# Scatters in pairs with work between them, and a final sum taken in another order

## The chip, the cores and the metric

The kernel runs on one core of a Trainium2 chip, as one launch. The metric is device time in microseconds (us). The engines are TensorE (PE; its weight loads are PEld), VectorE (DVE), ScalarE (ACT), GpSimd (POOL) and SyncE (SP, which only issues DMAs here). They run side by side, each in its own program order, and wait for each other by semaphores.

## The reference

The input x is 4 batches of 256 tokens of 256 values, all f32. Two layers follow, each with a layer norm before and behind it and a residual sum:

```
x = x + layernorm(attention(layernorm(x)))          16 heads of 128, rope, causal softmax
x = x + layernorm(experts(layernorm(x)))
experts(x): logits = x @ router.T + bias; the best 4 of 16 experts per token, weights by softmax
            out = sum over those 4 of weight * (down(gated(gate_up(x))) + down_bias)
layernorm(x) = (x - mean) / sqrt(var + 1e-5)        over the 256 values of a token
```

## The kernel before

Attention runs first, batch by batch and head by head (64 slots `n`). The expert layer works on tiles of 128 rows, one expert each. Which tokens go to which expert is only known at run time, so the kernel sorts rows in DRAM.

**Scatter.** For each of the 8 tiles of 128 tokens, GpSimd issues four indirect DMAs (`scatter(t, k)`, L530) that write the normalised rows `xrow` into `rows_d`, sorted by expert. Tiles 0 to 5 are scattered during attention, one or two DMAs per head. Tiles 6 and 7, the last batch, are scattered by eight DMAs in a row after attention.

**Tiles.** There are 47 expert tiles. The first 9 (`EARLY`) are full already without the last batch and are planned early. The others need the table of the last batch: VectorE works it out in `plan_tiles` (L1105 to L1122), TensorE turns it (L1519), VectorE stores it (`table_out`, L1126). SyncE then waits for that table and for all 32 scatters before it loads tile 9 (`load_rows`, L456). For each tile TensorE turns the rows (`turn_tile`, L1528), multiplies by the gate and up weights (`gate_up`, L1544) and by the down weights (`down`, L1563). ScalarE copies the turned rows (`xgT_out`, through the helper at L649), copies half of the weights into `gu_now` (also L649), applies the gelu (L759) and weighs the result into a ring `y` of 6 buffers (`weigh`, L777). VectorE copies the other half of the weights (`place_gu`, L1146, which waits for the `gate_up` of two tiles before), and does the clamping (L1156, L1162) and the product (L1172).

**Sums.** GpSimd adds each `y` tile into one of two DRAM sums by an accumulating indirect DMA (`add_rows(i)`, L625), tiles in turn into the first and the second. Each waits until the add before it in the same sum has landed. The last three tiles are not sent to DRAM: TensorE adds them from SBUF with selection matrices (`add_late`, L1678).

**End.** SyncE loads the two sums into `sum_a` and `sum_b`, in four pieces of two token tiles (L487, `u` = 0 to 3). TensorE adds them to the late tiles in PSUM by an identity product (`add_sum`, L1684). VectorE takes mean and variance (`row_stats`, L937 to L944), GpSimd makes the reciprocal deviation and the shift -mean/deviation (`power`, L506, L508), VectorE scales and adds x (`finish`, L1324), and ScalarE adds the shift (`shift_result`, L911). Then the output DMAs go, the last one from ScalarE's queue (L917). The residual x needs a shift of its own from the first layer; ScalarE adds it between tiles 13 and 16 (`shift_x`, L709).

Of the kernel before, what the change touches and what calls it, by code (L numbers as in the profile page):

```python
# [17 lines left out]
ALU = mybir.AluOpType  # L18
ACT = mybir.ActivationFunctionType
# [22 lines left out]
XG, XT, AR, YR, SUMS, LATE = 14, 2, 3, 6, 2, 3  # L42
# [5 lines left out]
def block_kernel(nc, x_d, wq_d, wk_d, wv_d, wo_d, rw_d, rb_d, gu_d, gub_d, dn_d, dnb_d,  # L48
                 rope_cos_d, rope_sin_d, mask_d, ident_d, out_d):
    ctx = ExitStack()  # L50
    with ctx:
# [3 lines left out]
        def sem(name):  # L55
            return ctx.enter_context(nc.semaphore(name))
# [120 lines left out]
        result = sum_a  # L177
# [54 lines left out]
        dve_token = sem("dve_token")  # L232
        pe_sum = sem("pe_sum")
# [10 lines left out]
        pool_table = sem("pool_table")  # L244

# [22 lines left out]
        dve_var = sem("dve_var")  # L268
        dve_xT = sem("dve_xT")
# [97 lines left out]
        def _(sp):  # L367
# [120 lines left out]
            for u in range(3):  # L488
                sp.wait_ge(act_moe, 2 * u + 2)
                sp.dma_start(out_rows[:, 2 * u:2 * u + 2, :], result[:, 2 * u:2 * u + 2, :]).then_inc(dma_out, 16)  # L490
            sp.wait_ge(act_moe, TILES - 1)
            sp.dma_start(out_rows[:, TILES - 2, :], result[:, TILES - 2, :]).then_inc(dma_out, 16)
# [4 lines left out]
        def _(pool):  # L497
# [3 lines left out]
            def power(kind, u):  # L501

                n = NORMS.index((kind, u))
                cols = slice(2 * n, 2 * n + 2)
                pool.wait_ge(dve_var, n + 1)
                pool.tensor_tensor(rstd[:, cols], var_eps[:, cols], minus_half[:, :], ALU.pow).then_inc(pool_rstd, 1)  # L506
                pool.wait_ge(pool_rstd, n + 1)
                pool.tensor_tensor(shift[:, cols], minus_mean[:, cols], rstd[:, cols], ALU.mult).then_inc(pool_shift, 1)  # L508
# [20 lines left out]
            def scatter(t, k):  # L529
                pool.indirect_dma_start(out=rows_d, out_offset=bass.IndirectOffsetOnAxis(  # L530
                    ap=slot_of[:, t, k:k + 1].bitcast(U32), axis=0), in_=xrow[:, t, :], in_offset=None).then_inc(dma_scatter, 16)
# [96 lines left out]

            power("a", B - 1)
            power("b", B - 1)  # L630
            may_scatter(B - 1)
            for t in (6, 7):
                for k in range(TOP):
                    scatter(t, k)
            pool.wait_ge(dma_start, 16 * (B - 1))
            for i in range(EARLY):
                add_rows(i)
# [9 lines left out]
        def _(sc):  # L647
# [246 lines left out]
            for i in range(EARLY, TILE_MAX + 2):  # L894
                if i + 1 < TILE_MAX:
                    experts[i + 1] = place_gu(i + 1)
                    xgT_out(i + 1)
                if i < TILE_MAX:
                    gelu(i)
                if i > EARLY:  # L900
                    weigh(i - 2, experts[i - 2])
                if EARLY + 4 <= i < EARLY + 8:
                    shift_x(i - EARLY - 4)

            def shift_result(u):

                n = NORMS.index(("moe", u))
                sc.wait_ge(pool_shift, n + 1)
                sc.wait_ge(dve_out, u + 1)
                for i in range(2):  # L910
                    sc.activation(result[:, 2 * u + i, :], result[:, 2 * u + i, :], ACT.Identity,  # L911
                                  bias=shift[:, 2 * n + i:2 * n + i + 1]).then_inc(act_moe, 1)

            for u in range(4):
                shift_result(u)
            sc.wait_ge(act_moe, TILES)
            sc.dma_start(out_rows[:, TILES - 1, :], result[:, TILES - 1, :]).then_inc(dma_out, 16)  # L917
# [3 lines left out]
        def _(dve):  # L921
# [8 lines left out]
            def row_stats(src, kind, u, first=None):  # L930
# [12 lines left out]
                dve.tensor_scalar(minus_mean[:, cols], mean_var[:, tiles, 0], -1.0, None, ALU.mult)  # L943
                dve.tensor_scalar(var_eps[:, cols], mean_var[:, tiles, 1], EPS, None, ALU.add).then_inc(dve_var, 1)  # L944

# [372 lines left out]
            def finish(u):  # L1318

                n = NORMS.index(("moe", u))  # L1320
                dve.wait_ge(pool_rstd, n + 1)
                dve.wait_ge(act_x, u + 1)
                for i in range(2):
                    m = dve.scalar_tensor_tensor(out=result[:, 2 * u + i, :], in0=ps_sum[u][:, i * M:(i + 1) * M],  # L1324
                                                 scalar=rstd[:, 2 * n + i:2 * n + i + 1], in1=x[:, 2 * u + i, :],
                                                 op0=ALU.mult, op1=ALU.add)
                m.then_inc(dve_out, 1)

            for u in range(4):
                dve.wait_ge(pe_sum, u + 1)  # L1330
                row_stats(ps_sum[u][:, :].rearrange("p (s m) -> p s m", s=2), "moe", u, 0)
                if u:
                    finish(u - 1)
            finish(3)


        @block.tensor
        def _(pe):
# [350 lines left out]
            for j in range(LATE - 1):  # L1689
                for u in range(4):  # L1690
                    add_late(u, j, first=j == 0)
            for u in range(4):
                add_late(u, LATE - 1)
                pe.wait_ge(dma_first[u], 16)
                add_sum(u, sum_a)
                pe.wait_ge(dma_second[u], 16)
                add_sum(u, sum_b, last=True).then_inc(pe_sum, 1)
# [37 lines left out]
```

## Time and profile before

| | before |
|---|---|
| median of 3 runs | 497.1 us (496.76 to 497.86) |
| profiled execution | 498.67 us |
| its span, first to last instruction | 496.7 us |
| PE busy | 470.8 us (95%) |
| DVE busy | 359.4 us (72%) |
| ACT busy | 326.9 us (66%) |
| POOL busy | 240.9 us (49%) |
| granted TensorE clock, mean | 0.988 |

Busy shares are means over stages. The clock column of the profile gives what the throttle granted, as a share of full speed: 1.00 is 2.4 GHz, 0.50 is 1.2 GHz. A row of the timeline gives start and duration in us, and in brackets how long the engine sat idle before it and what ended that. "remote" and "unknown queue" mean that the releaser could not be found among the instructions that ended then.

### The profile page before, as it was taken

The page shows a single profiled execution, that of the slowest core. Times are in us where ns is not written, and L with a number is a line of the kernel's source. Part 1 is how long each engine was busy: PE and PEld are TensorE (multiplying, and loading weights), DVE is VectorE, ACT ScalarE, POOL GpSimd, SP SyncE. Part 2 cuts the span into 40 slices and gives each one's busy share as a digit, 9 for nine tenths or more (in the row PEclk, how much of TensorE's full clock was granted, in tenths as well). Part 3 has the DMA queues.
Part 4 walks back from the last instruction along what each step waited for, and adds up shares of the span by engine and source line. Part 5 has one row for each costly group of instructions (what it writes and reads, how often), then busy time and mean ns, then how long its engine had stood idle before and what let it go on. Part 6 is the DMA issues. An engine that isn't in the chain of part 4 may idle for free. (4 is left out here: it accounts for less than half of the span.)

```text
span 496.7 us, 11704 instructions
## 1 busy us (share of the span) xinstructions
PE 470.8 (95%) x3482; PEld 439.7 (89%) x3482; DVE 359.4 (72%) x1263; ACT 326.9 (66%) x815; POOL 240.9 (49%) x228
## 2 busy tenths in 40 slices
PE   7799999999999999999999999998699999999993
PEld 4698899999999999999999998887589999999983
DVE  3798799687876677787678698577367778866735
ACT  4878986767676777667678566675256765665612
POOL 2888785435323256344453236115435565665612
PEclk9999999999999999999999999999799999999998
DMA  8367751999300000001365346631275665776462
GB/s 255 105 197 231 227 175 49 373 368 370 108 1 1 23 14 37 36 14 38 131 221 197 128 145 215 204 88 71 46 160 93 103 97 98 116 123 79 46 188 86
DMA packets 61661, 65.26 MB, mean 131 GB/s; under 512 B 4960, under 2 KB 56480, under 8 KB 61600
## 3 DMA queue, kind: packets, MB, share of 16 engines
q1 hardware_dynamic: 53008, 53.44, 33.6%
q0 software_dynamic: 7872, 10.49, 12.7%
q8 instruction: 30, 0.49, 0.4%
q10 hardware_dynamic: 720, 0.59, 0.4%
q14 instruction: 31, 0.25, 0.2%
HBM read 31.58 MB, written 32.92 MB: 130 GB/s over the span
## 5 line engine op out<-in xcount | busy, mean ns | idle before, releaser
L527 POOL TENSOR_TENSOR by_sin<-by_sin,rope_sin 128x512 f32<-128x512 f32 x64 | 82.8, 1294 | 139.9 <-ACT by_sin L649 139.9
L1343 PE MATMUL bank<-xT_parts,qk_h 128*128 128x256 f32 x512 | 99.6, 293 | 3.8 <-POOL qk_l L512 1.6
L1544 PE MATMUL bank<-xgT,gu_now 128*128 128x128 f32 x752 | 94.1, 279 | 7.2 <-DVE gu_now L1146 6.3
L1544 PEld LDWEIGHTS bank<-xgT,gu_now 128*128 128x128 f32 x752 | 89.4, 195 | 8.9 <-DVE gu_now L1146 7.0
L649 ACT ACTIVATE by_sin<-bank 64x512 f32<-64x512 f32 x128 | 75.9, 593 | 31.8 <-PE bank L1343 29.0
L625 POOL DMA_INDIRECT sum_d<-y,xg x44 | 69.9, 1589 | 55.0 <-ACT y L777 35.8
L1343 PEld LDWEIGHTS bank<-xT_parts,qk_h 128*128 128x128 f32 x512 | 79.1, 191 | 5.0 <-POOL qk_l L512 2.4
L671 ACT ACTIVATE prob<-score,row_bias 128x128 f32<-128x128 f32 (+1 forms) x128 | 57.0, 447 | 26.7 <-DVE row_bias L974 26.4
L1343 PE MATMUL bank<-xT_parts,qk_l 128*128 128x256 f32 x256 | 72.4, 283 | 0.0
L1343 PE MATMUL bank<-wv_h,xT_parts 128*128 128x256 f32 x256 | 66.6, 324 | 1.5 <-ACT V L649 1.4
L964 DVE TENSOR_TENSOR qkT<-bank,by_sin 128x512 f32<-128x512 f32 x64 | 44.3, 692 | 18.0 <-POOL by_sin L527 15.3
L974 DVE CUSTOM_DVE_ANT_0 score<-bank,mask 128x128 f32<-128x128 f32 (+1 forms) x128 | 40.3, 352 | 22.3 <-issue 22.1
L1563 PE MATMUL bank<-dn_w,act 128*128 x188 | 49.1, 386 | 0.2 <-DVE act L1172 0.2
L1343 PEld LDWEIGHTS bank<-wv_h,xT_parts 128*128 128x128 f32 x256 | 43.9, 189 | 5.8 <-ACT V L649 3.0
L1343 PEld LDWEIGHTS bank<-xT_parts,qk_l 128*128 128x128 f32 x256 | 48.8, 190 | 0.0
L956 DVE TENSOR_TENSOR bank<-bank,rope_cos 128x512 f32<-128x512 f32 x64 | 44.4, 694 | 2.2 <-ACT by_sin L649 2.0
L759 ACT ACTIVATE glu<-gate 128x256 f32<-128x256 f32 x47 | 19.5, 415 | 36.2 <-DVE gate L1156 33.8
L989 DVE TENSOR_TENSOR oT_l<-bank,oT_h 128x256 fp32r<-128x256 f32 x64 | 27.2, 425 | 21.7 <-ACT oT_h L649 21.3
L983 DVE TENSOR_SCALAR prob<-prob,row_rec 128x128 f32<-128x128 f32 (+1 forms) x128 | 41.2, 364 | 2.3
L530 POOL DMA_INDIRECT rows_d<-xrow,slot_of x32 | 32.6, 1020 | 15.4 <-DVE slot_of L1065 8.8
L1402 PE MATMUL bank<-probT,V 128*128 128x256 f32 x126 | 38.9, 390 | 0.9 <-ACT probT L649 0.9
L1156 DVE TENSOR_SCALAR gate<-bank,gate_bias 128x128 f32<-128x128 f32 x94 | 28.7, 346 | 13.7 <-PE bank L1544 8.8
(183 smaller groups left out, 1061.2 us busy)
## 6 DMA issues: line engine op xcount, KB each, us to landing
rows_d<-blank SPq DMA_DIRECT2D x32, 576.0 KB, 7.2
gu_w<-_L_ffn_gate_up_proj_dram SPq DMA_DIRECT2D x16, 512.0 KB
xg<-rows_d SPq DMA_DIRECT2D x47, 144.0 KB, 2.5
dn_w<-in_L_ffn_down_proj_dram SPq DMA_DIRECT2D x16, 256.0 KB
raw_qk<-in_L_attn_wq_dram SPq DMA_DIRECT2D x16, 128.0 KB, 3.6
raw_qk<-in_L_attn_wk_dram SPq DMA_DIRECT2D x16, 128.0 KB, 3.7
raw_v<-in_L_attn_wv_dram SPq DMA_DIRECT2D x8, 256.0 KB, 2.9
raw_o<-in_L_attn_wo_dram SPq DMA_DIRECT2D x16, 128.0 KB, 2.7
```

The costliest lines, as they stand in the source:

```text
L527: pool.tensor_tensor(v, v, rope_sin[:, :].unsqueeze(1).broadcast_to([P, 2, T]), ALU.mult).then_inc(pool_sin, 1)
L625: pool.indirect_dma_start(out=sum_d[HOME[i]], out_offset=bass.IndirectOffsetOnAxis(ap=xg[:, i % XG, TOKEN:TOKEN + 1].bitcast(U32), axis=0) ...
L649: return sc.activation(out, in_, ACT.Copy)
L671: e = sc.activation(prob[:, n % 2, lo:hi], score[:, n % 2, lo:hi], ACT.Exp, bias=row_bias[:, n % 2, i:i + 1], scale=-1.0, accum_out=row_su ...
L956: dve.tensor_tensor(v, v, rope_cos[:, :].unsqueeze(1).broadcast_to([P, 2, T]), ALU.mult).then_inc(dve_cos, 1)
L964: dve.tensor_tensor(qkT[:, n % QR, :, :].rearrange("p w t -> p (w t)"), ps_qk[n % 2][:, :], by_sin[:, n % 2, :], ALU.add).then_inc(dve_rop ...
L974: m = dve.tensor_tensor_reduce(score[:, n % 2, lo:hi], ps_s[:, lo:hi], mask[:, P:T] if i == 0 else mask[:, :], -1.0 / D, FILL, ALU.add, AL ...
L983: m = dve.tensor_scalar(prob[:, n % 2, lo:hi], prob[:, n % 2, lo:hi], row_rec[:, n % 2, i:i + 1], None, ALU.mult)
L1343: m = pe.matmul(out, lhs, rhs, start=first and i == 0, stop=last and i == len(terms) - 1, skip_group_check=not (first and last))
L1402: pe.matmul(ps_oT[n][:, 0:T], V[:, v, 0, a * D:(a + 1) * D], turned[n][:, 0:T], start=True, stop=False, skip_group_check=True)
L1544: m = pe.matmul(ps_gu[i][:, (2 * s + r) * P:(2 * s + r + 1) * P], gu_now[:, i % 2, k, s, r * P:(r + 1) * P], xgT[:, i % XT, k, :], start=( ...
L1563: m = pe.matmul(ps_out[i][:, 0:M], act[:, i % AR, r, :], dn_w[:, bass.ds(e, 1), r, :].rearrange("p o m -> p (o m)"), start=(r == 0), stop= ...
```

## The change

1. The eight scatters of the last batch go out in pairs. Behind each pair GpSimd adds the first layer's shift to one tile of x (tiles 0 to 3). Tiles 4 and 5 follow behind the first and the second `add_rows`. ScalarE keeps the shift of tiles 6 and 7 only.
2. The ring `y` has 8 buffers in place of 6.
3. At the end VectorE adds `sum_a` and `sum_b` in SBUF (four additions of 128x512), and TensorE adds one sum in place of two. All the products of the late tiles are issued before that.
4. ScalarE scales and shifts the sum from PSUM into `sum_b`, and then VectorE adds x. Before, VectorE scaled and added x, and then ScalarE shifted. The statistics of pieces 0 to 2 come before the first addition of x.
5. In every `row_stats` the variance is made before the negated mean, and GpSimd waits for the two by semaphores of their own.

```diff
-XG, XT, AR, YR, SUMS, LATE = 14, 2, 3, 6, 2, 3
+XG, XT, AR, YR, SUMS, LATE = 14, 2, 3, 8, 2, 3
@@ SyncE: the output DMAs wait for dve_out and send sum_b
-                sp.wait_ge(act_moe, 2 * u + 2)
-                sp.dma_start(out_rows[:, 2 * u:2 * u + 2, :], result[:, 2 * u:2 * u + 2, :]).then_inc(dma_out, 16)
+                sp.wait_ge(dve_out, 2 * u + 2)
+                sp.dma_start(out_rows[:, 2 * u:2 * u + 2, :], sum_b[:, 2 * u:2 * u + 2, :]).then_inc(dma_out, 16)
@@ GpSimd
                 pool.wait_ge(pool_rstd, n + 1)
+                pool.wait_ge(dve_mean, n + 1)
                 pool.tensor_tensor(shift[:, cols], minus_mean[:, cols], rstd[:, cols], ALU.mult).then_inc(pool_shift, 1)
+            def shift_x(t):
+                n = NORMS.index(("a", t // 2))
+                pool.wait_ge(pool_shift, n + 1)
+                pool.tensor_scalar(x[:, t, :], x[:, t, :], shift[:, 2 * n + t % 2:2 * n + t % 2 + 1], None, ALU.add).then_inc(pool_x, 1)
             may_scatter(B - 1)
-            for t in (6, 7):
-                for k in range(TOP):
-                    scatter(t, k)
+            scatter(6, 0)
+            scatter(6, 1)
+            shift_x(0)
+            scatter(6, 2)
+            scatter(6, 3)
+            shift_x(1)
...
             pool.wait_ge(dma_start, 16 * (B - 1))
-            for i in range(EARLY):
+            add_rows(0)
+            shift_x(4)
+            add_rows(1)
+            shift_x(5)
+            for i in range(2, EARLY):
                 add_rows(i)
@@ ScalarE
-                if EARLY + 4 <= i < EARLY + 8:
-                    shift_x(i - EARLY - 4)
+                if i == EARLY + 4:
+                    shift_x(B - 1)
-            def shift_result(u):
+            def scale_result(u):
                 n = NORMS.index(("moe", u))
                 sc.wait_ge(pool_shift, n + 1)
-                sc.wait_ge(dve_out, u + 1)
+                sc.wait_ge(pe_sum, u + 1)
+                sc.wait_ge(dve_two, u + 1)
                 for i in range(2):
-                    sc.activation(result[:, 2 * u + i, :], result[:, 2 * u + i, :], ACT.Identity,
-                                  bias=shift[:, 2 * n + i:2 * n + i + 1]).then_inc(act_moe, 1)
+                    sc.activation(sum_b[:, 2 * u + i, :], ps_sum[u][:, i * M:(i + 1) * M], ACT.Identity,
+                                  bias=shift[:, 2 * n + i:2 * n + i + 1],
+                                  scale=rstd[:, 2 * n + i:2 * n + i + 1]).then_inc(act_moe, 1)
@@ VectorE
-                dve.tensor_scalar(minus_mean[:, cols], mean_var[:, tiles, 0], -1.0, None, ALU.mult)
                 dve.tensor_scalar(var_eps[:, cols], mean_var[:, tiles, 1], EPS, None, ALU.add).then_inc(dve_var, 1)
+                dve.tensor_scalar(minus_mean[:, cols], mean_var[:, tiles, 0], -1.0, None, ALU.mult).then_inc(dve_mean, 1)
+            def add_two(u):
+                dve.wait_ge(dma_first[u], 16)
+                dve.wait_ge(dma_second[u], 16)
+                tiles = slice(2 * u, 2 * u + 2)
+                dve.tensor_tensor(sum_a[:, tiles, :], sum_a[:, tiles, :], sum_b[:, tiles, :], ALU.add).then_inc(dve_two, 1)
+            def add_x(u):
...
+                for i in range(2):
+                    dve.wait_ge(act_moe, 2 * u + i + 1)
+                    dve.tensor_tensor(sum_b[:, 2 * u + i, :], sum_b[:, 2 * u + i, :], x[:, 2 * u + i, :], ALU.add).then_inc(dve_out, 1)
-                if u:
-                    finish(u - 1)
-            finish(3)
+            for u in range(4):
+                add_two(u)
+            moe_stats(0)
+            moe_stats(1)
+            moe_stats(2)
+            add_x(0)
+            moe_stats(3)
+            for u in range(1, 4):
+                add_x(u)
@@ TensorE
             pe.wait_ge(act_xgT, TILE_MAX)
-            for j in range(LATE - 1):
+            for j in range(LATE):
                 for u in range(4):
                     add_late(u, j, first=j == 0)
             for u in range(4):
-                add_late(u, LATE - 1)
-                pe.wait_ge(dma_first[u], 16)
-                add_sum(u, sum_a)
-                pe.wait_ge(dma_second[u], 16)
-                add_sum(u, sum_b, last=True).then_inc(pe_sum, 1)
+                pe.wait_ge(dve_two, u + 1)
+                add_sum(u, sum_a, last=True).then_inc(pe_sum, 1)
```

GpSimd's instructions around the last batch's scatters (`rows_d`), before:

```order
L506 TENSOR_TENSOR rstd<-var_eps,minus_half 128x2
L508 TENSOR_TENSOR shift<-minus_mean,rstd 128x2
L530 DMA rows_d<-xrow,slot_of 16512x288 x8
L625 DMA sum_d<-y,xg 1152x256 x44
```

and now, from the same place on:

```order
L533 DMA rows_d<-xrow,slot_of 16512x288 x2
L636 TENSOR_SCALAR x<-x,shift 128x256
L533 DMA rows_d<-xrow,slot_of 16512x288 x2
L636 TENSOR_SCALAR x<-x,shift 128x256
L533 DMA rows_d<-xrow,slot_of 16512x288 x2
L636 TENSOR_SCALAR x<-x,shift 128x256
L533 DMA rows_d<-xrow,slot_of 16512x288 x2
L636 TENSOR_SCALAR x<-x,shift 128x256
L628 DMA sum_d<-y,xg 1152x256
L636 TENSOR_SCALAR x<-x,shift 128x256
L628 DMA sum_d<-y,xg 1152x256
```

Three shifts now stand ahead of the last scatter, four ahead of the first add into a DRAM sum (`sum_d`), and six ahead of the third.

VectorE's last instructions before (the statistics of pieces 2 and 3 and what follows each):

```order
L937 BN_STATS stats<-bank 128x6 x2
L940 BN_AGGR mean_var<-stats 128x2 x2
L943 TENSOR_SCALAR minus_mean<-mean_var 128x2
L944 TENSOR_SCALAR var_eps<-mean_var 128x2
L1324 SCALAR_TENSOR_TENSOR sum_a<-bank,rstd,x 128x256 x2
L937 BN_STATS stats<-bank 128x6 x2
L940 BN_AGGR mean_var<-stats 128x2 x2
L943 TENSOR_SCALAR minus_mean<-mean_var 128x2
L944 TENSOR_SCALAR var_eps<-mean_var 128x2
L1324 SCALAR_TENSOR_TENSOR sum_a<-bank,rstd,x 128x256 x4
```

and now (the row of four additions stands ahead of all statistics; behind the first piece's statistics, those of pieces 1 and 2 follow in the same form):

```order
L1347 TENSOR_TENSOR sum_a<-sum_a,sum_b 128x512 x4
L961 BN_STATS stats<-bank 128x6 x2
L964 BN_AGGR mean_var<-stats 128x2 x2
L967 TENSOR_SCALAR var_eps<-mean_var 128x2
L968 TENSOR_SCALAR minus_mean<-mean_var 128x2
...
L1357 TENSOR_TENSOR sum_b<-sum_b,x 128x256 x2
L961 BN_STATS stats<-bank 128x6 x2
L964 BN_AGGR mean_var<-stats 128x2 x2
L967 TENSOR_SCALAR var_eps<-mean_var 128x2
L968 TENSOR_SCALAR minus_mean<-mean_var 128x2
L1357 TENSOR_TENSOR sum_b<-sum_b,x 128x256 x6
```

The additions of the two sums come first, the additions of x follow the statistics, and x of the last piece is the last thing that VectorE does, where ScalarE's shift was last before.

## Rows read from the trace of the kernel before

**Rows 1.** Windows: PE, PEld, DVE, ACT, POOL busy us (instructions), clock, DMA, GB/s.

```profile
352.00:356.00 4.00, 3.54 (x16) 3.57 (x17) 1.36 (x5) 1.24 (x3) 1.60 (x1) 0.50 0.20 28
356.00:360.00 4.00, 4.00 (x16) 2.52 (x14) 0.43 (x1) 1.56 (x4) 0.76 (x1) 0.67 0.27 31
```

**Rows 2.** Timeline of PE: start, us, engine, line, what, xcount [idle before, releaser].

```profile
341.85 0.38 PE L1528 MATMUL bank<-ident,xg 128*128 128x128 f32 x2
345.09 2.02 PE L1544 MATMUL bank<-xgT,gu_now 128*128 128x128 f32 x16 [2.00 <-DVE gu_now L1146]
352.46 3.76 PE L1544 MATMUL bank<-xgT,gu_now 128*128 128x128 f32 x16 [4.27 <-DVE gu_now L1146]
```

**Rows 3.** Timeline of DVE and ACT in the same stretch.

```profile
344.52 0.43 DVE L1146 COPY gu_now<-gu_w 128x512 f32 x1 [1.67 <-remote]
...
351.83 0.38 ACT L649 ACTIVATE xgT<-bank 128x256 f32<-128x256 f32 x1 [3.21 <-remote]
```

**Rows 4.** Timeline of POOL, 338 to 360 us.

```profile
338.53 1.19 POOL L530 DMA_INDIRECT rows_d<-xrow,slot_of  x1 [8.82 <-DVE slot_of L1065]
...
347.91 0.96 POOL L530 DMA_INDIRECT rows_d<-xrow,slot_of  x1 [0.30 <-issue]
349.39 1.61 POOL L625 DMA_INDIRECT sum_d<-y,xg  x1 [0.52 <-issue]
...
359.24 1.57 POOL L625 DMA_INDIRECT sum_d<-y,xg  x1 [3.83 <-ACT y L777]
```

**Rows 5.** Timeline of POOL, an earlier pair of scatters.

```profile
296.42 0.96 POOL L530 DMA_INDIRECT rows_d<-xrow,slot_of  x1 [0.30 <-issue]
```

**Rows 6.** Windows around those pairs, columns as in rows 1.

```profile
295.00:300.00 5.00, 5.00 (x41) 4.86 (x41) 4.74 (x18) 2.93 (x8) 3.80 (x4) 1.00 0.53 190
```

**Rows 7.** Groups by form: busy us, mean ns of one.

```profile
L560 POOL TENSOR_SCALAR up_to<-up_to 128x256 f32<-128x256 f32 x1 | 0.9, 856 | 0.0
```

**Rows 8.** Windows, columns as in rows 1.

```profile
350.00:350.50 0.50, 0.00 (x0) 0.00 (x0) 0.00 (x0) 0.00 (x0) 0.50 (x1) 1.00 0.00 0
```

**Rows 9.** Timeline of DVE, SP and PE: the table and tile 9.

```profile
360.13 0.41 DVE L1126 CAST table<-bank 1x256 int32<-1x256 f32 x1 [2.31 <-PE bank L1519]
...
361.30 2.93 SPq L456 DMA_DIRECT2D xg<-rows_d  x3
...
365.06 0.44 PE L1528 MATMUL bank<-ident,xg 128*128 128x128 f32 x2 [0.70 <-DMA xg<-rows_d]
```

**Rows 10.** Groups by form of DVE.

```profile
L1040 DVE TENSOR_TENSOR earlier<-earlier,chosen 128x16 f32<-128x16 f32 x4 | 2.8, 693 | 0.1
...
L1041 DVE TENSOR_TENSOR earlier<-earlier,chosen 128x16 f32<-128x16 f32 x4 | 0.7, 176 | 0.1
```

**Rows 11.** The tile sum_b, 470 to 497 us: issues and landings.

```profile
L487 SPq DMA_DIRECT2D sum_b<-sum_d x4: 360/469/475, 476.8 to 478.2; - x4
DMA to landing us min/median/max: 4.6/5.0/5.3
```

**Rows 12.** Groups by form of DVE.

```profile
L1130 DVE TENSOR_TENSOR qk_l<-raw_qk,qk_h 128x512 fp32r<-128x512 f32 x2 | 1.4, 687 | 2.8 <-ACT qk_h L649 2.8
...
L1114 DVE TENSOR_TENSOR below<-tiles_of,up_to 128x256 f32<-128x256 f32 x1 | 0.4, 418 | 0.0
```

**Rows 13.** Timeline of PE, DVE, POOL and ACT at the end.

```profile
488.10 1.03 PE L1684 MATMUL bank<-sum_b,ident 128*128 128x256 f32 x4
...
484.75 0.76 DVE L937 BATCH_NORM_STATS2 stats<-bank 128x6 f32<-128x256 f32 x2 [0.95 <-PE bank L1684]
...
485.92 0.87 DVE L1324 SCALAR_TENSOR_TENSOR sum_a<-bank,rstd,x 128x256 f32<-128x256 f32 x2
...
486.09 0.69 POOL L506 TENSOR_TENSOR rstd<-var_eps,minus_half 128x2 f32<-128x2 f32 x1 [1.20 <-DVE var_eps L944]
...
486.88 0.91 ACT L911 ACTIVATE sum_a<-sum_a,shift 128x256 f32<-128x256 f32 x2 [10.42 <-DVE sum_a L1324]
...
493.13 0.36 ACTq L917 DMA_DIRECT2D out_dram<-sum_a  x1
```

More of the change, by code:

```diff
@@ L176, in block_kernel @@
         sum_b = sb("sum_b", [P, TILES, M])
-        result = sum_a
         turn = sb("turn", [P, LATE, TILES, P], F32R)
@@ L232, in block_kernel @@
         dve_token = sem("dve_token")
+        dve_two = sem("dve_two")
         pe_sum = sem("pe_sum")
@@ L244, in block_kernel @@
         pool_table = sem("pool_table")
+        pool_x = sem("pool_x")
         act_norm = sem("act_norm")
@@ L268, in block_kernel @@
         dve_var = sem("dve_var")
+        dve_mean = sem("dve_mean")
         dve_xT = sem("dve_xT")
@@ L488, in _ @@
             for u in range(3):
-                sp.wait_ge(act_moe, 2 * u + 2)
-                sp.dma_start(out_rows[:, 2 * u:2 * u + 2, :], result[:, 2 * u:2 * u + 2, :]).then_inc(dma_out, 16)
-            sp.wait_ge(act_moe, TILES - 1)
-            sp.dma_start(out_rows[:, TILES - 2, :], result[:, TILES - 2, :]).then_inc(dma_out, 16)
+                sp.wait_ge(dve_out, 2 * u + 2)
+                sp.dma_start(out_rows[:, 2 * u:2 * u + 2, :], sum_b[:, 2 * u:2 * u + 2, :]).then_inc(dma_out, 16)
+            sp.wait_ge(dve_out, TILES - 1)
+            sp.dma_start(out_rows[:, TILES - 2, :], sum_b[:, TILES - 2, :]).then_inc(dma_out, 16)
             sp.wait_ge(dma_out, 16 * 5)
@@ L631, in _ @@
             may_scatter(B - 1)
-            for t in (6, 7):
-                for k in range(TOP):
-                    scatter(t, k)
-            pool.wait_ge(dma_start, 16 * (B - 1))
-            for i in range(EARLY):
+            scatter(6, 0)
[4 more added lines that the diff above has]
+            shift_x(1)
+            scatter(7, 0)
+            scatter(7, 1)
+            shift_x(2)
+            scatter(7, 2)
+            scatter(7, 3)
+            shift_x(3)
+            pool.wait_ge(dma_start, 16 * (B - 1))
+            add_rows(0)
[3 more added lines that the diff above has]
+            for i in range(2, EARLY):
                 add_rows(i)
@@ L901, in _ @@
                     weigh(i - 2, experts[i - 2])
-                if EARLY + 4 <= i < EARLY + 8:
-                    shift_x(i - EARLY - 4)
-            def shift_result(u):
+                if i == EARLY + 4:
+                    shift_x(B - 1)
+            def scale_result(u):
                 n = NORMS.index(("moe", u))
                 sc.wait_ge(pool_shift, n + 1)
-                sc.wait_ge(dve_out, u + 1)
+                sc.wait_ge(pe_sum, u + 1)
+                sc.wait_ge(dve_two, u + 1)
                 for i in range(2):
-                    sc.activation(result[:, 2 * u + i, :], result[:, 2 * u + i, :], ACT.Identity,
-                                  bias=shift[:, 2 * n + i:2 * n + i + 1]).then_inc(act_moe, 1)
+                    sc.activation(sum_b[:, 2 * u + i, :], ps_sum[u][:, i * M:(i + 1) * M], ACT.Identity,
+                                  bias=shift[:, 2 * n + i:2 * n + i + 1],
+                                  scale=rstd[:, 2 * n + i:2 * n + i + 1]).then_inc(act_moe, 1)
             for u in range(4):
-                shift_result(u)
-            sc.wait_ge(act_moe, TILES)
-            sc.dma_start(out_rows[:, TILES - 1, :], result[:, TILES - 1, :]).then_inc(dma_out, 16)
+                scale_result(u)
+            sc.wait_ge(dve_out, TILES)
+            sc.dma_start(out_rows[:, TILES - 1, :], sum_b[:, TILES - 1, :]).then_inc(dma_out, 16)
         @block.vector
@@ L1316, in _, with moe_stats @@
                 late_low(j, experts[LAST + j])
[L1318 to L1322, printed above, removed]
-                for i in range(2):
[L1324 to L1329, printed above, removed]
+            def add_two(u):
[4 more added lines that the diff above has]
+            def add_x(u):
+                if u < B - 1:
+                    dve.wait_ge(pool_x, 2 * u + 2)
+                else:
+                    dve.wait_ge(act_x, 1)
+                for i in range(2):
+                    dve.wait_ge(act_moe, 2 * u + i + 1)
+                    dve.tensor_tensor(sum_b[:, 2 * u + i, :], sum_b[:, 2 * u + i, :], x[:, 2 * u + i, :], ALU.add).then_inc(dve_out, 1)
+            def moe_stats(u):
                 dve.wait_ge(pe_sum, u + 1)
                 row_stats(ps_sum[u][:, :].rearrange("p (s m) -> p s m", s=2), "moe", u, 0)
-                if u:
-                    finish(u - 1)
-            finish(3)
+            for u in range(4):
[7 more added lines that the diff above has]
+                add_x(u)
         @block.tensor
```

## The prediction

> **What bounds the kernel now.** I read the chain of waits first, from 400 us to the end. It is one engine almost without a gap: each expert tile costs TensorE 1.79 us for the gate and up products, 0.87 us down and 0.22 us for the turn, 2.87 us in all. A change to VectorE, ScalarE or GpSimd inside these 38 tiles is worth nothing unless it makes TensorE wait. So I looked for the places where the chain leaves TensorE. There are two, and the change touches both: the last batch's sorting (338 to 365 us), and the end behind the last tile (472 us on).
>
> In the first place the timeline of TensorE shows two waits for `gu_now`, 2.00 and 4.27 us [rows 2], and behind the second the sixteen products take 3.76 us where 2.02 are usual [rows 2], because the granted clock is 0.50, the 1.2 GHz level [rows 1]. The reader should see what is odd in the waits. TensorE turned tile 6 at 341.85 [rows 2], and its `gate_up(5)` stood ahead of that; yet VectorE, which needs only `gate_up(5)` for its next copy, starts at 344.52, and the releaser is "remote" [rows 3]. In the second wait ScalarE's copy of turned rows starts at 351.83 after 3.21 us idle, again "remote" [rows 3]. TensorE had done its part some 2 to 4.5 us before; its signals came late, and only its. This stretch is the one in which GpSimd issues nine indirect DMAs with gaps of 0.30 to 0.52 us, from 338.53 to 351.00 [rows 4]. During attention scatters also went out in pairs 0.30 us apart [rows 5], four pairs with a 128x512 product between them, and there TensorE was busy without a gap [rows 6]. No row shows the cause; the unbroken run of scatters is what differs. The runs without a profile are no shorter than the profiled one by more than 1.6 us, so I take the waits to be in them as well.
>
> **Profiled against timed.** The profiled execution took 498.67 us, 1.97 us outside its span of 496.7; the median is 497.1, 1.57 us less. I work out differences in the profiled execution and take them off the median.
>
> **Scatters in pairs.** A GpSimd tensor_scalar of 128x256 took 0.86 us [rows 7]. It splits a gap of 0.30 us in two of about 0.17, so each shift moves what follows by 0.9 us (1.16 if both gaps stay at 0.30). Three shifts stand ahead of the last scatter: its issue ends at 348.87 + 2.7 = 351.6 (at most 352.4). Nothing is moving on the DMA engines 1.1 to 1.6 us after that issue [rows 8], so it has landed 1.3 us after, at 352.9. The fourth shift and then the first `add_rows` follow: it moves from 349.39 to about 353, and the second goes at 355.6. The third waits for ScalarE's y and went at 359.24 [rows 4]; with two more shifts GpSimd is free at 358.2, so the chain of adds is not late from there on. If TensorE's waits stay as they are, all of this costs nothing: SyncE waits for the table, which VectorE stores until 360.54, and issues tile 9 at 361.30 [rows 9].
>
> If the waits go, TensorE gains 2.00 + 4.27 and half of the time at the lower clock: all of 352 to 356 and 2.6 us of the next four (a mean of 0.67) [rows 1], with a little before 352 some 6.8 us, half of it 3.4; together 9.7 us: the table would be stored at 350.9. Then the scatters end last: 352.9 + 0.76 (from table to first issue, 361.30 - 360.54 [rows 9]) = 353.7 for tile 9's load. It moves forward by 361.3 - 353.7 = 7.6 us, and everything from 365.06 on with it [rows 9]. The bounds are 6.8 us (shifts at 1.16) and 9.7 us. What is late next is this load: TensorE has finished tiles 6 to 8 at about 354.4 and waits until 357.4. After a wait of 4.27 us its clock was at 0.50; if 3 us also bring that about, 3.4 us are lost again.
>
> The shifts also meet VectorE. Two additions of the same 128x16 form take 693 ns in one line and 176 ns in the next [rows 10]: 0.52 us each for something other than work, with GpSimd's products running beside them. The Trainium skill, SBUF — State Buffer, section on the two separate sides, says that GpSimd and a VectorE operation with two SBUF inputs, or in a two-port mode, take a shared pair of ports as a lock, and the later one waits for the whole instruction. By that rule each of the four shifts can hold VectorE's planning of the table or its copy of weights for up to 0.86 us, 3.4 in all. By the trace's own number it is 4 x 0.52 = 2.1 us, against a slack of 352.9 - 350.9 = 2.0 us before the table matters: I count nothing. By the skill's rule at its worst the table is 1.4 us behind the scatters, and the time 1.4 us more.
>
> **The ring of 8.** ScalarE waits for a landing of `y` nowhere in the chain, and GpSimd, one add in 1.9 us where TensorE makes a tile in 2.87, catches up. Nothing, from either side. **ScalarE's six shifts gone:** 0.5 us each beside TensorE's tiles. Nothing. **Variance before mean:** `power` starts 0.08 us sooner; it counts once, at the end.
>
> **The end.** The pieces of `sum_b` are issued from 476.76 to 478.2 and land after 4.6 to 5.3 us, from 481.34 to 483.5 [rows 11]. VectorE's addition of 128x512 is 0.69 us [rows 12] and follows each landing: done at 484.2. TensorE's take of the last sum, 1.03 us as at 488.10 [rows 13], ends at 485.3 and not 489.13. So TensorE wins 3.8 us, but VectorE now starts its statistics at 484.2 and is the bound. A block of statistics is 485.92 - 484.75 = 1.17 us [rows 13]. Three blocks, to 487.8; the first addition of x, twice about 0.38 at a cadence below the 418 ns of this form [rows 12], to 488.5; the fourth block, to 489.7. GpSimd's power starts 0.09 later (486.09 against 486.00, [rows 13]), 0.69 + 0.08 + 0.20, ScalarE from 490.8 for 0.91 [rows 13], to 491.7; the last addition of x ends at 492.2, where the output's DMA went at 493.13 [rows 13]. The gain is 0.9 us. Bounds: 0.3 (each of six hand-overs 0.1 dearer) and 1.5 (the pieces land as fast as the median 5.0 allows, and ScalarE reads PSUM as fast as SBUF).
>
> **Sum.** 497.1 - 7.6 - 0.9 = 488.6.
>
> **Rivals.** *A: the waits stay.* For it: no row names their cause, and ten DMAs of GpSimd still go out in one stretch. Against: the four pairs without a wait. Then only the end counts: 497.1 - 0.9 = 496.2, of which half a chance lies on either side of what can be told. *B: one wait goes.* The run of scatters is looser, and TensorE's signals are held once: if the shorter one goes, 497.1 - 2.0 - 0.9 = 494.2. *C, slower: the hold ends with the run.* It ended at 351.8, 0.8 us after GpSimd's first add was issued (349.39 + 1.61). If any run of indirect DMAs at this density holds the signals until it ends, the first add now ends at 354.6, the hold at 355.4: 3.6 us later, 497.1 + 3.6 - 0.9 = 499.8. It decides if pairs 1.2 us apart count as one run; the pairs of attention stood 2.1 us and more apart, so they don't exclude it. *D: the clock falls in the new wait of 3 us:* 488.6 + 3.4 = 492.0, inside the first case.
>
> **Chances.** Forecast (waits gone, D included) 0.45; B 0.10; A 0.26; C 0.14; other mishaps 0.05. The forecast's own range is 487 to 492; the whole range 487 to 497 holds it with A and B, 0.81. What a measurement tells from no change is about 0.2%, 1.0 us. Faster: 0.45 + 0.10 + 0.11 of A = 0.66; no change 0.15; slower 0.19.
>
> **What would show it.** In the profile after: no "remote" wait of ScalarE or VectorE between 338 and 356 us and no slice of lower clock there; tile 9's load issued near 353.7, released by a scatter and not by the table; tile-by-tile 2.87 us as before; at the end VectorE without a gap from the first addition to the last statistics, TensorE idle, and the last DMA 0.9 us nearer to the landing of `sum_b`. The forecast is wrong if waits of the same kind stand there still, wherever they have moved, or if GpSimd's shifts take well over 0.86 us.

## The result

| | median us | runs | ratio to before, 95% |
|---|---|---|---|
| before | 497.47 (496.76 to 497.86) | 4 | |
| changed | 493.73 (493.23 to 493.98) | 4 | 0.9926 [0.9907, 0.9944] |

The kernel became faster by 3.7 us, where 8.5 were forecast. The profiled execution went from 498.67 to 493.98 us, its span from 496.7 to 491.9. The time of 493.7 lies inside the whole range and above the forecast's own (487 to 492).

The sorting first. The page's line of the granted clock has one lower slice left ahead of the last, near 360 us, and the windows of the changed kernel (columns as in rows 1) show where it is:

```profile
PEclk9999999999999999999999999999989999999997
```

```profile
342.00:345.00 3.00, 3.00 (x25) 2.74 (x24) 2.24 (x7) 1.76 (x5) 2.52 (x3) 1.00 0.26 98
348.00:352.00 4.00, 3.96 (x26) 2.86 (x25) 3.22 (x14) 1.65 (x4) 3.38 (x4) 1.00 0.22 85
352.00:356.00 4.00, 2.81 (x18) 2.25 (x16) 2.80 (x10) 2.12 (x5) 3.79 (x4) 1.00 0.19 65
356.00:360.00 4.00, 1.29 (x6) 1.08 (x7) 1.60 (x2) 1.30 (x4) 3.65 (x4) 0.87 0.86 207
360.00:364.00 4.00, 4.00 (x28) 4.00 (x27) 0.99 (x4) 0.58 (x2) 2.75 (x2) 0.71 0.86 186
```

In the windows from 342 to 345 and from 348 to 352 TensorE is busy almost without a gap, at full clock: both waits of [rows 2] are gone, and the list of waits from 338 to 358 us has no "remote" in it. What is late instead is seen in 356:360, where it is busy for 1.29 us of 4. Its timeline in the changed kernel says for what it waits:

```profile
343.32 2.02 PE L1582 MATMUL bank<-xgT,gu_now 128*128 128x128 f32 x16
352.92 1.89 PE L1601 MATMUL bank<-dn_w,act 128*128 x8
357.19 0.41 PE L1566 MATMUL bank<-ident,xg 128*128 128x128 f32 x2 [2.38 <-issue]
359.12 0.69 PE L1566 MATMUL bank<-ident,xg 128*128 128x128 f32 x2 [1.52 <-DMA xg<-rows_d]
359.60 3.26 PE L1582 MATMUL bank<-xgT,gu_now 128*128 128x128 f32 x16
```

First the rows of tile 9, then those of tile 10. After the two waits the sixteen products take 3.26 us where 2.02 are usual: the granted clock is 0.50 for 3.4 us from 358.9 on, the 1.2 GHz level. Tile 10's turn stood at 365.06 before [rows 9] and is 5.9 us earlier; tile 11's, behind the slow products, is only 4.8 us earlier (367.49 to 362.69).

GpSimd's timeline, changed kernel, from the first scatter to the first add and the shift behind it (start, us, line, what, [idle before]):

```profile
338.92 1.19 POOL L533 DMA_INDIRECT rows_d<-xrow,slot_of  x1 [8.79 <-DVE slot_of L1089]
...
341.62 0.96 POOL L636 TENSOR_SCALAR x<-x,shift 128x256 f32<-128x256 f32 x1
...
346.48 1.32 POOL L533 DMA_INDIRECT rows_d<-xrow,slot_of  x1 [0.17 <-issue]
...
351.65 0.97 POOL L533 DMA_INDIRECT rows_d<-xrow,slot_of  x1 [0.30 <-issue]
...
353.77 1.84 POOL L628 DMA_INDIRECT sum_d<-y,xg  x1 [0.17 <-issue]
355.11 1.49 POOL L636 TENSOR_SCALAR x<-x,shift 128x256 f32<-128x256 f32 x1
```

and SyncE's load of tile 9, 361.30 before [rows 9]:

```profile
355.05 2.77 SPq L458 DMA_DIRECT2D xg<-rows_d  x3
```

The last scatter's issue ends at 352.62, SyncE is released at 354.12, and the table had been stored at 351.76. So the load is released by the scatter and not by the table, as forecast, but 1.35 us later than forecast.

The end, changed kernel: VectorE's additions, the last statistics' GpSimd steps, ScalarE, the last addition of x and the last DMA (rows 13 for before).

```profile
476.07 1.43 DVE L1347 TENSOR_TENSOR sum_a<-sum_a,sum_b 128x512 f32<-128x512 f32 x2 [3.60 <-DMA sum_b<-sum_d]
...
478.58 1.40 DVE L1347 TENSOR_TENSOR sum_a<-sum_a,sum_b 128x512 f32<-128x512 f32 x2 [1.08 <-DMA sum_b<-sum_d]
...
485.29 0.87 POOL L508 TENSOR_TENSOR rstd<-var_eps,minus_half 128x2 f32<-128x2 f32 x1 [0.68 <-DVE var_eps L967]
486.23 0.43 POOL L511 TENSOR_TENSOR shift<-minus_mean,rstd 128x2 f32<-128x2 f32 x1
486.70 1.02 ACT L934 ACTIVATE sum_b<-bank,shift,rstd 128x256 f32<-128x256 f32 x2 [1.04 <-POOL shift L511]
487.36 0.81 DVE L1357 TENSOR_TENSOR sum_b<-sum_b,x 128x256 f32<-128x256 f32 x2 [0.75 <-ACT sum_b L934]
488.21 0.37 ACTq L941 DMA_DIRECT2D out_dram<-sum_b  x1
```

The last add into the DRAM sum lands at 473.21 (476.75 before), and from there to the last DMA it takes 15.00 us where it took 16.38.

### The profile page after: what moved, and what is told of

It reads as the page before. It is cut to its first block and busy times, and to the rows that moved or that the text cites. A ratio compares the mean times of both kernels' runs of the same rounds, so it can differ in the third digit from the quotient of the medians.

```text
span 491.9 us, 11694 instructions
## 1 busy us (share of the span) xinstructions
PE 466.0 (95%) x3466; PEld 435.9 (89%) x3466; DVE 362.3 (74%) x1267; ACT 325.3 (66%) x809; POOL 248.3 (50%) x234
```

## The experiments

The experiments ran in four groups. Each group ran on one chip beside the kernel before, and the chips turned out to matter. The changed kernel ran in every group but that of chip 15.

| chip | before, median us (range, runs) |
|---|---|
| first comparison | 497.47 (496.76 to 497.86, 4) |
| 15 (e1 to e4) | 498.01 (493.44 to 500.00, 35) |
| 5 (e5 to e8) | 490.15 (488.44 to 492.93, 21) |
| 5 (e9 to e12) | 490.05 (488.78 to 493.26, 29) |
| 0 (e13 to e16) | 497.64 (495.81 to 500.17, 17) |

The same program takes 7.3 to 8.0 us less on chip 5. So each ratio below is to before on its own chip.

How late TensorE's signals are is read as follows: TensorE turns the rows of a tile, and ScalarE copies them. In e9, where nothing is late, the copy starts 0.04 us after the end of the turn; in the first profile of before it starts 2.23 us after the second turn of this stretch and 4.50 us after the third.

### e1: the middle alone

Before, with the pairs and GpSimd's shifts; the ring stays at 6, the end is the old one.

```diff
-            for t in (6, 7):
-                for k in range(TOP):
-                    scatter(t, k)
+            scatter(6, 0)
+            scatter(6, 1)
+            shift_x(0)
...
```

> Only the middle of the change (pairs of scatters with shifts on GpSimd), ring of 6, the end as before. My theory: the whole of the 3.7 us gain but the end's share comes from here, since the late signals of TensorE go: 0.5 to 0.7% below before (about 494 to 495 us), no remote wait between 338 and 356 us. Rival (the end made the gain): within 0.2% of before. Rival (the ring of 8 matters): ScalarE waits for a landing of y in the tiles.

Measured (chip 15): 498.09 us, 1.001 [0.998, 1.004]. Both waits of TensorE are gone (one signal is still 0.8 us late, but TensorE has work for that long), and tile 9's load goes at 355.31. But nothing is won. Its list of waits from 350 to 366 us (who waited for what: us in total, times, longest), and TensorE's row:

```profile
ACT y L797 <- DMA sum_d<-y,xg: 6.8, 2, 5.0
```

```profile
362.79 3.75 PE L1567 MATMUL bank<-xgT,gu_now 128*128 128x128 f32 x16 [3.13 <-ACT xgT L669]
```

GpSimd's first adds now go out behind the scatters and shifts, and ScalarE finds no free buffer of `y`; the turned rows behind that copy are late and TensorE waits. Its clock is at 0.50 for 6.8 us. Tile 11's turn is at 366.34, where the changed kernel has 362.69.

### e2: the end alone

Before, with the changed end; scatters in a row, ring of 6.

```diff
+            for u in range(4):
+                add_two(u)
+            moe_stats(0)
...
```

> Only the end of the change, with the eight scatters in one row, the ring of 6 and the six shifts on ScalarE as before. My theory: 0.9 to 1.5 us below before (496.0 to 496.6), and the two remote waits of 2 to 4 us still stand between 341 and 352 us. Rival: the end makes the whole gain, 3.7 us.

Measured (chip 15): 496.03 us, 0.9969 [0.9942, 0.9995]. The late signals stand as before (1.46 and 5.21 us), the load goes at 359.26. From the issue of the last add to the last DMA it takes 19.84 us, in the first profile of before 20.96.

### e3: the row of eight back

The changed kernel, the eight scatters in a row, then the four shifts.

```diff
-            scatter(6, 0)
...
+            for t in (6, 7):
+                for k in range(TOP):
+                    scatter(t, k)
+            for t in range(4):
+                shift_x(t)
```

> The changed kernel with the eight scatters in one row again and the first four shifts behind them. My theory (an unbroken row of scatters delays TensorE's signals): the waits of 2 and 4 us return, tile 9's load is issued near 361 us, and the time is 3 to 4 us above the changed kernel, about 497. Rival (the waits were chance, or due to something else that the change moved): no waits, and tile 9 earlier by up to 2 us than in the changed kernel since the scatters end sooner, 491 to 493.

Measured (chip 15): 496.13 us, 0.9976 [0.9951, 1.0001]. TensorE's timeline has both waits again:

```profile
344.66 2.02 PE L1575 MATMUL bank<-xgT,gu_now 128*128 128x128 f32 x16 [1.95 <-ACT xgT L664]
...
350.69 3.34 PE L1575 MATMUL bank<-xgT,gu_now 128*128 128x128 f32 x16 [2.93 <-ACT xgT L664]
```

The second wait is shorter than before (4.27), and the load goes at 358.25. The four shifts (4.06 us) stand here between the last scatter and the first add, where the add followed at once; how long the signals are held seems to depend on where the run of indirect DMAs ends, the add included. No run tests this by itself. The ratio's interval does not meet those of the changed kernel on the first chip and on chip 0 (0.9926 and 0.9921).

### e4: a memset between the pairs

The changed kernel, but between the pairs only a `memset` of 128x32, which clears an unused buffer; the shifts go behind the adds.

```diff
+                    if k % 2 == 1:
+                        pool.memset(gap[:, 2 * t + k // 2 - 12, :], 0.0)
```

> The changed kernel, but between the pairs only a memset of 32 values (0.1 us), the shifts behind the first six adds. If any GpSimd instruction between the pairs is enough to break the row: no late signals, the last scatter some 2.5 us sooner, tile 9's load near 352.5 to 353.5, and 1 to 3 us below the changed kernel. If the mean rate of scatters decides (one in 1.33 us against 1.86): the waits return in whole or part, and the time is near 496 to 498.

Measured (chip 15): 496.77 us, 0.9973 [0.9946, 1.0000]. GpSimd between two pairs, and TensorE:

```profile
342.05 0.14 POOL L646 MEMSET gap<- 128x32 f32 x1
342.36 0.97 POOL L534 DMA_INDIRECT rows_d<-xrow,slot_of  x1 [0.17 <-issue]
```

```profile
353.30 3.75 PE L1574 MATMUL bank<-xgT,gu_now 128*128 128x128 f32 x16 [4.97 <-ACT xgT L663]
```

The memset fits into the gap that is there anyway: from the end of one pair's issue (342.05) to the next it is 0.31 us, as between the scatters of the row (0.30). The signals are 1.5 and 5.2 us late. So an operation between the pairs that leaves no pause does not help; the run does not tell what a short pause would do.

### e5: the changed kernel once more

No edit.

> The changed kernel itself, once more beside before on this chip. If the 0.74% of the first comparison is the change's: 0.6 to 0.9% below before again, no remote wait in the profile, a clock dip of 3.4 us or none behind tile 9. If that was chance of a chip or a profile: within 0.3% of before.

Measured (chip 5): 493.61 us, 1.0058 [1.0034, 1.0081]. The changed kernel takes the same time as at first; the kernel before is what is faster here, and the change costs 3.5 us.

### e6: the ring of 6

```diff
-XG, XT, AR, YR, SUMS, LATE = 14, 2, 3, 8, 2, 3
+XG, XT, AR, YR, SUMS, LATE = 14, 2, 3, 6, 2, 3
```

> The changed kernel with the ring y of 6 buffers. My new theory (the late adds of GpSimd make ScalarE wait for a landing of y where the ring is 6, which keeps tile 10's turned rows from TensorE and costs it 3.1 us idle and a clock dip of 6.8 us): 3 to 5 us above the changed kernel of the same call, ScalarE waiting for sum_d by some 5 us. My forecast's view (the ring is worth nothing): equal to the changed kernel within 0.2%.

Measured (chip 5): 496.39 us, 1.0123 [1.0097, 1.0149], 2.8 us over e5. ScalarE's wait for a landing of `y` is back as in e1 and the clock is at 0.50 for 6.8 us instead of 3.4. The ring is worth 2.8 us once the adds start late.

### e7 and e14: an idle wait between the pairs

GpSimd waits for the pair to land (1.74 us) and does nothing; the shifts go behind the adds. e14 is the same kernel on another chip.

```diff
+                    if k % 2 == 1 and (t, k) != (7, 3):
+                        pool.wait_ge(dma_scatter, 16 * (4 * t + k + 1))
```

> The changed kernel with no shift between the pairs: GpSimd waits idle for the landing of each pair (some 1.3 us) and the shifts stand behind the adds. If the pause between indirect DMAs is what keeps TensorE's signals on time: no late signals, last scatter and tile 9's load about as in the changed kernel (355). If GpSimd's own work in SBUF between them matters: the signals are late by 2 to 5 us as in the row of eight.

Measured (chip 5): 494.72 us, 1.0082 [1.0055, 1.0110]. On this chip the row of eight has no late signals either (e9, e10), so e7 tells nothing of their cause.

> The idle wait for landings in place of the shifts between the pairs, on what I hope is a chip with late signals (before at 497 or more). If the pause is what keeps the signals on time: none late, 494 to 495 us. If GpSimd's work in SBUF is: late signals again, 497 or more. If before takes 490 here, this run tells nothing of it.

Measured (chip 0): 494.46 us, 0.9925 [0.9902, 0.9949]. GpSimd, and the window in which before has its first wait:

```profile
343.02 0.96 POOL L533 DMA_INDIRECT rows_d<-xrow,slot_of  x1 [1.74 <-DMA rows_d<-xrow,slot_of]
```

```profile
342.00:345.00 3.00, 3.00 (x25) 2.77 (x24) 2.15 (x8) 2.12 (x5) 1.67 (x2) 1.00 0.20 75
```

Signals are late by 1.2 us at most, and TensorE loses 0.40 us to them. The pause alone removes nearly all of the hold, and GpSimd needs no work in it. That GpSimd's work in SBUF adds nothing is not shown: the pauses with shifts are shorter (1.2 to 1.4 us) and leave at most 0.8 us (e13).

### e8: tile 10 turned later

The changed kernel; TensorE makes half of tile 9's gate and up products before it turns tile 10, and so doesn't wait for tile 10's rows.

```diff
+            gate_up(EARLY, [0])
+            turn_tile(EARLY + 1)
+            gate_up(EARLY, [1])
```

> The changed kernel, but TensorE starts the products of tile 9 before it turns tile 10, whose rows land 1.9 us later than tile 9's. Theory (in the changed kernel this wait of 1.5 us and the clock dip behind it hold the end): 1.0 to 2.5 us below the changed kernel, first products of tile 9 at about 358.2 where they were at 359.6. Rival (tile 10's rows hold it all the same, one step on): within 0.5 us of it.

Measured (chip 5): 492.95 us, 1.0046 [1.0027, 1.0065]. TensorE behind the first wait:

```profile
358.50 1.13 PE L1582 MATMUL bank<-xgT,gu_now 128*128 128x128 f32 x8 [0.67 <-DVE gu_now L1170]
...
360.58 0.38 PE L1566 MATMUL bank<-ident,xg 128*128 128x128 f32 x2
```

Eight products in 1.13 us are at full clock; there is no dip. Tile 11's turn is at 360.58, in e5 at 363.14. Of these 2.6 us the medians show 0.7, which the two intervals don't tell from nothing; the profiled execution was 1.5 us below e8's own median, so it may not stand for the others.

### e9: the kernel before, profiled on chip 5

No edit; this run separates the chip from the change.

> The kernel before itself, for a second profile. The medians of before in the three calls so far were 497.5, 498.0 and 490.2 us. Theory (TensorE's late signals come or stay away by chip, not by kernel): on a chip where before takes 490 the profile shows no remote wait between 338 and 356 us and no clock dip there, and tile 9's load at about 353; on a chip where it takes 497 or more, the waits are there. Rival (the 7 us lie elsewhere, in attention or in the DMAs): the row of scatters looks the same in both.

Measured (chip 5): 490.51 us, 1.0002 [0.9978, 1.0026]. GpSimd's last scatter stands at the very time of [rows 4]:

```profile
347.89 0.96 POOL L530 DMA_INDIRECT rows_d<-xrow,slot_of  x1 [0.30 <-issue]
```

but TensorE's timeline and windows show neither wait:

```profile
342.97 2.05 PE L1544 MATMUL bank<-xgT,gu_now 128*128 128x128 f32 x16
...
350.61 2.02 PE L1544 MATMUL bank<-xgT,gu_now 128*128 128x128 f32 x16
...
356.69 0.44 PE L1528 MATMUL bank<-ident,xg 128*128 128x128 f32 x2 [1.76 <-DMA xg<-rows_d]
```

```profile
342.00:345.00 3.00, 3.00 (x25) 2.69 (x24) 2.08 (x7) 2.08 (x5) 2.39 (x3) 1.00 0.30 114
```

and the table and the load follow:

```profile
350.90 0.41 DVE L1126 CAST table<-bank 1x256 int32<-1x256 f32 x1
```

```profile
352.20 2.93 SPq L456 DMA_DIRECT2D xg<-rows_d  x3
```

Here the load goes at 352.20, and in e5 at 354.96: with no late signals to cure, the pairs only make the last scatter late. Behind the wait of 1.76 us for tile 10 the clock is at 0.50 for 3.4 us here too, from 357.9 on.

### e10: the end alone, on chip 5

The kernel of e2.

> The end alone once more (scatters in a row, ring of 6, shifts on ScalarE). Theory (the end gives 1 to 1.5 us on every chip): 0.2 to 0.35% below before. On a chip without late signals it is then the fastest of this call, 3 to 5 us below the changed kernel.

Measured (chip 5): 489.99 us, 1.0002 [0.9978, 1.0026]. The changed end alone brings nothing that can be told in the timed runs. In the profiles the way from the issue of the last add to the last DMA is 19.90 us here and 21.23 in e9. This is a second profile of the row of eight on chip 5, and its copies again start 0.04 us after the turns.

### e11: the changed kernel, third time

No edit.

> The changed kernel in the same call as the end alone. Theory: 493 to 494 us whatever the chip, since its pairs never show late signals; so below before by 0.7% where before has them, above it by 0.6% where not. Rival: its time moves with before's.

Measured (chip 5): 493.24 us, 1.0071 [1.0046, 1.0095].

### e12: the wait filled

e8, and 24 products whose result nobody reads while TensorE waits for tile 9.

```diff
+            keep_busy(ones[:, :], before[:, :], 12, out=bank[6])
```

> The changed kernel with tile 10 turned in the middle of tile 9's products, and twelve products of 128x128 that nobody reads (2.7 us) in TensorE's wait for tile 9. Theory (the clock falls behind that wait and costs up to 1.7 us more): no slice of lower clock, 1.0 to 3.0 us below the changed kernel. Rival (the fillers delay tile 9 as much as the clock gives): within 0.5 us of it.

Measured (chip 5): 491.66 us, 1.0028 [1.0001, 1.0055]. The filled stretch of TensorE:

```profile
356.17 2.84 PE L1552 MATMUL bank<-before,ones 128*128 128x128 f32 x24
```

There is no dip, as in e8. The median is 1.6 us below e11's; how much of that is the filling and how much the later turn of tile 10, which e8 had too, is not told apart. In this profile the scatters begin 1.1 us later than in e8's (340.27 and 339.13), so the two profiles can't be set against each other to the microsecond.

### e13: the changed kernel, fourth time

No edit.

> The changed kernel beside before once more. Theory (its time stays at 493 to 494 us; the sign of the change is before's): 0.7% below before if before takes 497 or more in this call, 0.6% above if it takes 490.

Measured (chip 0): 494.00 us, 0.9921 [0.9896, 0.9946]. The first result is there again. One signal is 0.74 us late in its profile, and TensorE has work for that long.

### e15: the row of eight with e8's order

A row of eight, the shifts behind the adds, and e8's order on TensorE.

```diff
+            for t in (6, 7):
+                for k in range(TOP):
+                    scatter(t, k)
...
+            gate_up(EARLY, [0])
+            turn_tile(EARLY + 1)
+            gate_up(EARLY, [1])
```

> The changed end and ring of 8, the eight scatters in one row, the shifts behind the adds, and tile 10 turned in the middle of tile 9's products. Theory: where before takes 490, this is the fastest, 487 to 489; where before takes 497 or more it has the late signals too and takes 495 to 497, so it beats before on both kinds of chip and the changed kernel on one.

Measured (chip 0): 497.89 us, 1.0001 [0.9979, 1.0024]. TensorE's second wait, and two lines of the list of waits:

```profile
352.94 3.46 PE L1571 MATMUL bank<-xgT,gu_now 128*128 128x128 f32 x16 [4.92 <-DVE gu_now L1159]
```

```profile
ACT xgT L660 <- remote: 3.9, 1, 3.9
DVE gu_now L1159 <- remote: 3.8, 2, 2.9
```

The ring of 8, the shifts on GpSimd, the new end and the later turn are all in it; without the pauses they win nothing that can be told.

### e16: fours

The changed kernel with four scatters, three shifts, four scatters, one shift.

```diff
+            for k in range(TOP):
+                scatter(6, k)
             shift_x(0)
...
+            for k in range(TOP):
+                scatter(7, k)
```

> The scatters in two fours with three shifts between (3 us). If late signals need more than two scatters in a row: on a chip where before takes 497 or more they show in each four, shorter than in the row of eight, 494 to 497 us. If it is the mean rate over the stretch that counts, which is the changed kernel's: none. Where before takes 490: none either way.

Measured (chip 0): 493.14 us, 0.9905 [0.9878, 0.9932]. The pause between the fours, and the window of the wait for tile 9:

```profile
344.74 3.21 POOL L636 TENSOR_SCALAR x<-x,shift 128x256 f32<-128x256 f32 x3
```

```profile
356.00:360.00 4.00, 1.60 (x7) 0.94 (x8) 2.92 (x7) 2.78 (x6) 3.82 (x4) 1.00 0.69 147
```

In the first four the signals are 1.4 us late, in the second 0.5. That moves some of TensorE's idle time ahead of the wait for tile 9, its clock stays at 1.00, and the time is as good as that of e13 or a little better; the intervals overlap.

## Why the prediction was right in kind and wrong in size

**The mechanism held, where there was something to cure.** The prediction said: "No row shows the cause; the unbroken run of scatters is what differs." In the same changed kernel the row of eight brings the waits back (e3, e15), a memset that leaves no pause keeps them (e4), pauses of 1.2 to 1.4 us (changed, e13) and 1.74 us (e14) take nearly all of them away. So on these chips the row of scatters makes TensorE's signals late and a pause ends it: that is shown. What passes between the engines meanwhile is not. Rivals A and B, waits that stay, fell. C, a hold that ends with the run of DMAs at 355, fell too: VectorE and ScalarE have no remote wait there.

**The prediction missed that the waits go with the chip.** "I take the waits to be in them as well" fits the first chip: before takes 497 to 498 us where a row of eight is seen to hold signals, 490.1 where e9 and e10 show no hold. (The ground it gave was misread: the shortest of the three timed runs was 1.9 us below the profiled one, not 1.6.) On chip 5, in two groups, the same row at the same time holds nothing up, and the change is a loss: 1.0058 and 1.0071 (e5, e11), 0.9926 and 0.9921 elsewhere. The changed kernel itself takes 493.2 to 494.0 us on all of them. One profile of before could not show this. e9 bears out the prediction's working of what a kernel without the waits does: "the table would be stored at 350.9", and VectorE's cast ends at 351.31 there, 9.2 us sooner where 9.7 were worked out.

**The failed step is the term of 7.6 us:** "It moves forward by 361.3 - 353.7 = 7.6 us, and everything from 365.06 on with it". In the profiled executions the load moved by 6.25, the tiles behind it by 4.8, and the landing of the last add by 3.5. The parts:
- Scatters and load, 1.35 us late. The first scatter began 0.39 later. Three shifts moved the last scatter's end by 3.36 - 2.7 = 0.66 more than forecast: a shift took 0.96 to 1.18 us and not 0.86, and one scatter 1.32. The landing took 1.5 us from the issue's end, not 1.3, and 0.1 lies behind it.
- Tile 10's rows, 0.3 us: "what is late next is this load" was said of tile 9; the load of tile 10 holds TensorE a second time, by 1.52 us.
- The clock, 1.1 us. This was rival D, put "inside the first case" and left out of its number. It should have been in: after 4.27 us idle the clock had been at 0.50 [rows 1, 2], and the new waits add up to 3.9. The sixteen products took 1.24 us more, where rival D priced the dip at 3.4. Where the second wait is shorter (e8) the dip is gone, but e16 has none behind 0.86 and 1.54 us and e9 has one behind 1.76, so these rows don't say which wait brings it.
- By the last add, 0.5 us of the tiles' gain is lost before its issue (467.88 for 472.17) and 0.75 in its landing (5.33 us for 4.57). Why is open: over e2, e5, e9, e10 and e13 the landing takes 4.0 to 5.2 us and does not follow the kernel.

With the end's 0.5 us more, 8.5 - 4.0 + 0.5 = 5.0, and the last DMA stands 4.9 us earlier. Of the 1.2 us from there to the measured 3.7, 0.95 lies between profile and median (before's profiled execution was 1.20 above its median, the changed one's 0.25), and 0.2 behind the last DMA and outside the span.

**"Nothing, from either side" for the ring of 8 was wrong.** I looked at the chain of before, where the adds begin at 349.39 [rows 4]. In the changed kernel they begin at 353.77, and with 6 buffers ScalarE stands for a landing: 2.8 us (e6), and in e1, by its profile, 3.6 us (tile 11's turn at 366.34 for 362.69), which is what the middle had to win. The rule to take from it: an edit that costs nothing in the old order must be priced in the new one.

**The end** was forecast at 0.9 us and is 1.38 in the profile. The last piece of `sum_b` landed 0.7 us sooner (6.0 us from the first issue, 6.7 forecast), the statistics took 0.2 less, and GpSimd's two small products 0.4 more: 0.87 and 0.43 us where they took 0.69 and 0.20 [rows 13]. VectorE's additions of x from SBUF run beside them now; the first product of pieces 0 and 1, which runs beside statistics, still takes 0.72 and 0.69. The Trainium skill, SBUF — State Buffer, section on the two separate sides, has the later of GpSimd and a VectorE operation with two SBUF inputs wait for the shared ports; these rows agree in direction (0.41 us in sum). In timed runs the end alone gave 0.3% on chip 15 (e2, interval from 0.05 to 0.6%) and nothing on chip 5 (e10), though both profiles show the end shorter by 1.1 and 1.3 us. Whether it is worth 1.4 us in timed runs is not settled.

**Not settled.** Why TensorE's signals come late in a row of scatters, and why on one chip of those seen they don't. The trace names the releaser only as "remote". That it is the chip, and not something else that changed between the groups, rests on one chip without the hold, seen in two groups, and on three with it. Pauses between 0.31 and 1.2 us were not tried.

No version tried beats both kernels on both kinds of chip: on chips with late signals e16, the changed kernel and e14 are best; on chip 5 it is the kernel before, which the new end alone (e10) equals and nothing betters.

## What to carry to other kernels

Where VectorE or ScalarE wait for TensorE although its part is done, look at what GpSimd issues in that stretch, and break a row of indirect DMAs by pauses of 1.2 us or more, filled with work if there is any. Run before and changed kernel on more than one chip before a change of 1% is believed: here the sign depended on it. And when an edit delays what empties a ring, count the buffers in the new order, and count the granted clock behind each new wait of TensorE.

## What the runs showed of the hardware

- The same program took 490.1 us on one chip and 497.5 to 498.0 in the comparisons on others, and its two profiles differ in TensorE's late signals: tile 9's load went at 352.20 and at 361.30.
- ScalarE's copy of turned rows started 0.04 us after the turn's end where nothing was late. On the first chip, on 15 and on 0, with eight scatters 0.30 us apart, two copies started 1.4 to 2.2 and 3.2 to 5.2 us after (before, e2, e3, e15); with a memset in that gap 1.5 and 5.2 (e4); with rows of four 1.4 and 0.5 (e16); with pauses of 1.74 us 0.6 (e14); with pauses of 1.2 to 1.4 us 0.8 at most (changed, e1, e13). On chip 5 it was 0.04 throughout the scatters in all eight profiles, two of them with the row of eight (e9, e10).
- GpSimd's tensor_scalar of 128x256 took 0.86 us alone, 0.93 to 1.20 between scatters, 1.49 overlapped with an add's issue.
- The clock fell behind some of TensorE's waits and not behind others: it stayed at 1.00 in e8 behind 2.23 and 0.67 us and in e16 behind 0.86 and 1.54; it was at 0.50 for 3.4 us in e9 behind 1.76 and in the changed kernel behind 2.38 and 1.52, and for 6.8 us in before behind 4.27.
